# Two re-orderings in a twelve-sublayer kernel: the next layer's statistics behind the turned probabilities, and the next rows turned between the two columns of the second expert product

## The chip, the cores and the metric

The kernel runs as one program on one core of a Trainium2 chip. The metric is the device time of one execution in microseconds (us). TensorE (PE) multiplies matrices, VectorE (DVE), ScalarE (ACT) and GpSimd (POOL) do elementwise work, and SyncE (SP) issues the DMA transfers. The engines run their own instruction streams in order and meet through semaphores. PEld is the loading of TensorE's stationary operand.

## The reference, cut to what matters

Twelve sublayers are added one after another to x, which has 64 x 32 = 2048 rows of 256 features. Two of them matter here. The fixed experts (sublayer 2) normalise x twice, project it, and send each row through one of eight expert networks, chosen by the row's position:

```python
x = x + _L0_ffn_ref(_layernorm(x, axis=-1), ...)    # sublayer 2, in words:
# f = normalised x;  a = f + attn_w(norm(f) * ln_scale + ln_bias) + attn_b
# h = gelu(a @ w1[e] + b1[e]);  o = h @ w2[e] + b2[e];  x += gelu(o @ next_w + next_b)
```

The complex attention (sublayer 4) is self-attention among the 32 rows of each of the 64 batches, with scores from products folded ahead of time:

```python
x = x + _L1_attn_ref(_layernorm(x, axis=-1), ...)   # sublayer 4, in words:
# t = xn @ m;  s = t xn^T + biases;  p = exp(scale*(s - max s));  z = xn @ n
# x += (p @ z) / sum(p) + output bias
```

Sublayer 5 begins with a layer norm of x again. Its mean and root are made row tile by row tile inside sublayer 4; these are the "next layer's statistics" of the title.

## The kernel before, in words

All of x lies in SBUF as 16 tiles of 128 rows. The sublayers run one after another, with a barrier and a new block of engine programs between two of them. Inside a sublayer every engine has a function `turn`, written out by hand, that is called for the first and the last tiles in straight code and for the others in a hardware loop. What stands first in a turn is done first on that engine, whatever is ready, so the order of the calls in `turn` is the schedule.

**Fixed experts** (`fixed_experts_ffn`, names begin with `l0f_`). A turn handles one of 8 experts, with two row tiles (u = 0 and 1) of 128 rows. In the turn of expert e, TensorE does the first layer of e (`first_layer`, 16 products into `ps_h`), turns the normalised rows of e+1 to features (`turn_normed`, four transposes for each u, all into one PSUM bank `ps_t`), does the second layer of e (`second_layer`, 16 products into `ps_e`: 8 for each of two 128-column halves oc), the projection of e+1 (`projection`, into `ps_a`) and the next projection of e (`next_projection`, into `ps_y`). ScalarE copies the turned rows out of `ps_t` (`keep_turned`, into `flatT` and `xn2T`), makes the gelus (`gelus`) and copies the second layer's output (`keep_expert_output`, into `eoT`). The bank `ps_t` is shared by u = 0 and u = 1, so `turn_normed(n, 1)` waits for `keep_turned(n, 0)`. `projection` waits for `keep_turned(n, 1)`. `next_projection` waits for `eoT`. VectorE makes `xaT` from the projection, and `first_layer` of the next turn waits for it.

**Complex attention** (`complex_attention`, names begin with `l1a_`). A turn handles one of 16 row tiles. TensorE in turn i: scores of tile i (`scores`), transposes of tile i+2 (`turn_xn`), projections of tile i+1, and the weighed rows of tile i (`weighed_rows`, which waits for the probabilities that VectorE has turned). VectorE in turn i: row maxima of the scores, statistics of the finished tile i-1 for the next layer (`next_norm`), statistics of tile i+3 (`norm_stats`), turned probabilities of tile i (`turn_probs`, after ScalarE's exp), the normalised tile i+3 (`normed`, which waits for the root that GpSimd makes from `norm_stats`), and the sum into x (`add_output`). GpSimd makes that root (`layer_norm_root`), then x plus bias, then the next layer's root (`next_root`) from what `next_norm` left. `normed` gives the tile that `turn_xn` transposes.

```python
wait(dve, s["x_done"], n)
nc.vector.bn_stats(next_stats[:], core.x[:, i, :]).then_inc(s["next_stats_ready"], 1)
after(dve, s["next_rstd_ready"], n - 1, alone=True)
wait(dve, s["next_stats_ready"], n)
nc.vector.bn_aggr(next_moments[:], next_stats[:]).then_inc(s["next_mean_ready"], 1)
```

Of the kernel before, what the change touches and what calls it, by code (L numbers as in the profile page):

```python
# [25 lines left out]
P = 128  # L26
D = 256
C = D // P
# [1169 lines left out]
def complex_attention(core, tag):  # L1198
# [4 lines left out]
    nc = core.nc  # L1203
# [4 lines left out]
    with ExitStack() as ctx:  # L1208
# [231 lines left out]
        @block.vector  # L1440
        def _(dve):
            def spread_bv():
                nc.vector.tensor_copy(bv_rows[:], bv.unsqueeze(2).broadcast_to([P, CE, P])).then_inc(s["bv_spread"], 1)

            def keep_products():
                dve.wait_ge(s["vectors_ready"], 1)
                nc.vector.tensor_copy(bias_product[:], ps_c)
                nc.vector.tensor_copy(u[:], ps_u)
                nc.vector.tensor_copy(w[:], ps_w).then_inc(s["vectors_kept"], 1)
                dve.wait_ge(s["n_ready"], 1)  # L1450
                nc.vector.tensor_copy(n_vo[:], ps_n[:]).then_inc(s["n_kept"], 1)

            def keep_output_bias():
                dve.wait_ge(s["output_bias_ready"], 1)
                nc.vector.tensor_tensor(output_bias[:], ps_bo, bo, ALU.add).then_inc(s["output_bias"], 1)

            def maxima(n):
                dve.wait_ge(s["scores_ready"], n)
                nc.vector.tensor_reduce(big[:], ps_s, X, ALU.max, negate=True).then_inc(s["max_ready"], 1)
                dve.wait_ge(s["max_ready"], n)  # L1460
                nc.vector.tensor_scalar(minus_big[:], big[:], float(scale), None, ALU.mult).then_inc(s["bias_ready"], 1)

            def turn_probs(n):
                dve.wait_ge(s["exp_ready"], n)

                after(dve, s["y_ready"], n - 1)
                nc.vector.transpose(probsT[:], probs[:]).then_inc(s["probs_turned"], 1)

                after(dve, s["x_done"], n - 1)
                nc.vector.reciprocal(rinv[:], rsum[:]).then_inc(s["inv_ready"], 1)  # L1470

            def add_output(i, n):
                dve.wait_ge(s["y_ready"], n)
                dve.wait_ge(s["x_biased"], n)
                dve.wait_ge(s["inv_ready"], n)
                nc.vector.scalar_tensor_tensor(core.x[:, i, :], ps_y, rinv[:], x_plus_bo[:], ALU.mult,
                                               ALU.add).then_inc(s["x_done"], 1)

            def next_norm(i, n):
# [7 lines that stand above are left out]
            def turn(i, par):  # L1487
                if there(i, 0):
                    maxima(i + 1)
                if there(i, -1):  # L1490
                    next_norm(i - 1, i)
                if there(i, 3):
                    norm_stats(dve, nc, s, i + 4, core.x[:, i + 3, :], stats[:], mean[:])
                if there(i, 0):
                    turn_probs(i + 1)
                if there(i, 3):

                    after(dve, s["xn_turned"], i + 3)
                    normed(dve, nc, s, i + 4, core.x[:, i + 3, :], xn[:], mean[:], rstd[:])
                if is_turn(i, -AHEAD):  # L1500
                    core.wait_for_pack(dve)
                    spread_bv()
                if is_turn(i, -2):
                    keep_products()
                if is_turn(i, -1):
                    keep_output_bias()
                if there(i, 0):
                    add_output(i, i + 1)

            all_turns(dve, turn)  # L1510
            next_norm(NT - 1, NT)

# [522 lines left out]
def fixed_experts_ffn(core, tag):  # L2035
# [3 lines left out]
    nc = core.nc  # L2039
    E, HID = 8, 4 * D  # L2040
    HC = HID // P
# [3 lines left out]
    with ExitStack() as ctx:  # L2045
# [56 lines left out]
        @block.tensor  # L2102
        def _(pe):
            def turn_normed(n, u):

                if u:
                    pe.wait_ge(half_read[u - 1], n)
                    pe.wait_ge(flat_read[u - 1], n)
                else:
                    after(pe, half_read[U - 1], n - 1)  # L2110
                    after(pe, flat_read[U - 1], n - 1)
                pe.wait_ge(ln[1][u]["xn_ready"], n)
                for c in range(C):
                    nc.tensor.transpose(ps_t[:, c, :], flat[:, u, c * P:c * P + P], ident)
                for c in range(C):
                    last = nc.tensor.transpose(ps_t[:, C + c, :], xn2[:, u, c * P:c * P + P], ident)
                last.then_inc(turned[u], 1)

            def projection(n):
                after(pe, s["xaT_ready"], n - 1)  # L2120
                pe.wait_ge(half_read[U - 1], n)
                for oc in range(C):
                    for c in range(C):
                        last = nc.tensor.matmul(ps_a[:, oc, :], attn_w[:, c, oc * P:oc * P + P], xn2T[:, c, :],
                                                start=(c == 0), stop=(c == C - 1))
                last.then_inc(s["attn_ready"], 1)

            def first_layer(n):
                pe.wait_ge(s["w1_loaded"], n * 32)
                pe.wait_ge(s["xaT_ready"], n)  # L2130
                for k in range(HC // 2):
                    after(pe, h_kept[k], n - 1)
                    for hc in (2 * k, 2 * k + 1):
                        for c in range(C):
                            last = nc.tensor.matmul(ps_h[:, k, hc % 2, :], w1[:, c, hc * P:hc * P + P], xaT[:, c, :],
                                                    start=(c == 0), stop=(c == C - 1))
                    last.then_inc(h_ready[k], 1)

            def second_layer(n):
                pe.wait_ge(s["w2_loaded"], n * 32)  # L2140
                after(pe, s["eoT_ready"], n - 1)
                for oc in range(C):
                    for hc in range(HC):
                        if oc == 0 and hc % 2 == 0:
                            pe.wait_ge(h_kept[hc // 2], n)
                        last = nc.tensor.matmul(ps_e[:, oc, :], w2[:, hc, oc * P:oc * P + P], hT[:, hc, :],
                                                start=(hc == 0), stop=(hc == HC - 1))
                last.then_inc(s["out_ready"], 1)

            def next_projection(n):  # L2150
                after(pe, s["y_kept"], n - 1)
                pe.wait_ge(s["eoT_ready"], n)
                for u in range(U):
                    for c in range(C):
                        last = nc.tensor.matmul(ps_y[:, u, :], eoT[:, c, u * P:u * P + P], next_w[:, c, :],
                                                start=(c == 0), stop=(c == C - 1))
                last.then_inc(s["y_ready"], 1)

            def turn(e, now, ahead, ahead2):
                if ahead and not now:  # L2160
                    core.wait_for_pack(pe)
                if now:
                    first_layer(e + 1)
                if ahead:
                    turn_normed(e + 2, 0)
                if now:
                    second_layer(e + 1)
                if ahead:
                    turn_normed(e + 2, 1)
                    projection(e + 2)  # L2170
                if now:
                    next_projection(e + 1)

            staged_tiles(pe, turn, E)

        @block.scalar
        def _(act):
# [40 lines left out]
            def turn(e, now, ahead, ahead2):  # L2218
                if now:
                    gelus(e + 1)  # L2220
                if ahead:
                    keep_turned(e + 2, 0)
                if now:
                    keep_expert_output(e + 1)
                if ahead:
                    keep_turned(e + 2, 1)
                if now:
                    act.wait_ge(s["y_kept"], e + 1)
                    nc.scalar.activation(y[:], y[:], ACT.Gelu).then_inc(s["gelu_ready"], 1)

# [1570 lines left out]
```

## Time and profile before

| what | value |
|---|---|
| time before, median of 3 runs | 3566.3 us (3560.57 to 3572.57) |
| the profiled execution, its own time | 3571.8 us |
| its span | 3570.0 us |
| PE busy in the span | 3298.9 us (92%) |
| PE weight loads | 2646.9 us (74%) |
| DVE busy | 2152.4 us (60%) |
| ACT busy | 1428.5 us (40%) |
| POOL busy | 1017.6 us (29%) |
| mean granted TensorE clock | 0.958 |

The profiled execution took 3571.8 us, of which 1.8 us lie outside its span. It is 5.5 us above the median of the runs. Shares are averages over twelve stages with different limits; the steady part of the fixed experts lies at about 375 to 517 us of the span, and that of the complex attention at about 1012 to 1073 us. Times in rows are in us from the span's start. A granted clock of 1.00 is TensorE's level of 2.4 GHz, 0.50 that of 1.2 GHz.

### The profile page before, as it was taken

To read this page: it belongs to the slowest core of one execution; us is meant where nothing else is said; L and a number is where in the kernel's file an instruction comes from. 1 tells how busy PE (TensorE), PEld (TensorE's weight loads), DVE (VectorE), ACT (ScalarE), POOL (GpSimd) and SP (SyncE) were. 2 spreads that over 40 slices of the span, in tenths; PEclk is the share of its full clock that TensorE was granted. 3 is DMA by queue.
4 is the path that set the end of the run, shared out by engine and by line. 5 is a ranking of instruction groups with operands and counts; after the bars stand their busy time and mean duration, and the time that the engine had idled before them with its cause. 6 is when DMAs were issued, how large, how long until landed. Compare 5 with 4: busy or idle time off the path is not lost. (4 is left out here: it accounts for less than half of the span.)

```text
span 3570.0 us, 105629 instructions
## 1 busy us (share of the span) xinstructions
PE 3298.9 (92%) x39322; PEld 2646.9 (74%) x39322; DVE 2152.4 (60%) x7124; ACT 1428.5 (40%) x4209; POOL 1017.6 (29%) x1587
## 2 busy tenths in 40 slices
PE   8988889999986999999999999887999999998799
PEld 6767777777765888888877777774666788878576
DVE  3766225555656888889645555763334566558545
ACT  2334335555532333333245555541111455555222
POOL 0112113333342444445333333442110111112421
PEclk9999999999997999999999999978999999999799
DMA  6653334212103000000041111033112411110323
GB/s 208 216 175 154 102 94 108 61 56 56 64 1 140 3 3 3 2 3 2 2 99 43 40 47 46 2 111 124 46 47 72 87 38 38 41 34 2 108 79 114
DMA packets 149258, 238.26 MB, mean 67 GB/s; under 512 B 14456, under 2 KB 121720, under 8 KB 147176
## 3 DMA queue, kind: packets, MB, share of 16 engines
q1 hardware_dynamic: 138816, 203.16, 18.2%
q0 software_dynamic: 10176, 31.47, 3.1%
q8 instruction: 177, 2.90, 0.4%
q14 instruction: 89, 0.73, 0.1%
HBM read 213.61 MB, written 38.94 MB: 71 GB/s over the span
## 5 line engine op out<-in xcount | busy, mean ns | idle before, releaser
L3299 POOL TENSOR_TENSOR l1fu_second_weighed<-l1fu_second,l1fu_parts 128x256 bf16<-128x256 bf16 x384 | 278.7, 753 | 339.2 <-DVE l1fu_second L3540 332.3
L3351 PEld LDWEIGHTS l1fu_ps_u<-l1f_xnT_all,l1f_key_in 128*128 128x128 f32 x2048 | 252.0, 195 | 17.3 <-issue 11.0
L3351 PE MATMUL l1fu_ps_u<-l1f_xnT_all,l1f_key_in 128*128 (+1 forms) x2048 | 254.9, 278 | 8.6 <-issue 5.5
L3362 PE MATMUL l1fu_ps_y<-l1f_key_out,l1fu_units 128*128 128x256 f32 x1024 | 250.6, 389 | 2.0 <-DVE l1fu_units L3548 2.0
L3362 PEld LDWEIGHTS l1fu_ps_y<-l1f_key_out,l1fu_units 128*128 128x128 f32 x1024 | 185.7, 190 | 33.6 <-issue 6.2
L3413 ACT COPY l1fu_plane<-l1fu_ps_p 128x512 f32<-128x512 f32 x128 | 75.1, 586 | 250.4 <-PE l1fu_ps_p L3341 250.4
L3535 DVE TENSOR_TENSOR l1fu_first<-l1fu_index,l1fu_counted 128x1024 bf16<-128x1024 bf16 x128 | 166.8, 1303 | 12.8 <-PE l1fu_ps_p L3341 9.6
L3421 ACT ACTIVATE l1fu_units<-l1fu_ps_u 128x512 f32<-128x512 f32 x128 | 76.6, 598 | 151.9 <-PE l1fu_ps_y L3362 139.9
L1020 ACT ACTIVATE l3x_scores<-l3x_scores,l3x_minus_big 128x257 f32<-128x257 f32 x256 | 129.0, 511 | 2.3 <-DVE l3x_minus_big L1109 2.3
L1020 ACT ACTIVATE l1x_scores<-l1x_scores,l1x_minus_big 128x257 f32<-128x257 f32 x256 | 128.9, 511 | 2.1 <-DVE l1x_minus_big L1109 2.1
L1020 ACT ACTIVATE l2x_scores<-l2x_scores,l2x_minus_big 128x257 f32<-128x257 f32 x256 | 128.8, 511 | 2.1 <-DVE l2x_minus_big L1109 2.1
L3007 DVE TENSOR_TENSOR l2f_hidden<-l2f_hidden,l2f_ps_u 128x512 f32<-128x512 f32 x55 | 37.8, 688 | 151.7 <-PE l2f_ps_u L2751 136.8
L3341 PE MATMUL l1fu_ps_p<-l1fu_second_weighed,l1fu_first 64*128 64x32 bf16 x6144 | 113.1, 191 | 10.2 <-POOL l1fu_second_weighed L3299 9.4
L854 PE MATMUL l2x_ps_kv<-weights,l2x_ctx_sb 128*128 128x256 f32 x488 | 121.6, 392 | 0.0
L854 PE MATMUL l3x_ps_kv<-weights,l3x_ctx_sb 128*128 128x256 f32 x488 | 121.6, 392 | 0.0
L854 PE MATMUL l1x_ps_kv<-weights,l1x_ctx_sb 128*128 128x256 f32 x488 | 121.6, 392 | 0.0
L844 PE MATMUL l2x_ps_kv<-l2x_ctx_sb,weights 128*128 128x256 f32 x496 | 119.1, 383 | 0.0
L844 PE MATMUL l3x_ps_kv<-l3x_ctx_sb,weights 128*128 128x256 f32 x496 | 118.6, 382 | 0.0
L844 PE MATMUL l1x_ps_kv<-l1x_ctx_sb,weights 128*128 128x256 f32 x496 | 118.4, 382 | 0.0
L3341 PEld LDWEIGHTS l1fu_ps_p<-l1fu_second_weighed,l1fu_first 64*128 64x128 bf16 x6144 | 98.3, 95 | 26.5 <-issue 12.9
L854 PEld LDWEIGHTS l3x_ps_kv<-weights,l3x_ctx_sb 128*128 128x128 f32 x488 | 87.7, 189 | 33.0 <-ACT l3x_kT L1013 12.0
L854 PEld LDWEIGHTS l2x_ps_kv<-weights,l2x_ctx_sb 128*128 128x128 f32 x488 | 87.7, 189 | 33.0 <-issue 12.0
(743 smaller groups left out, 8383.6 us busy)
## 6 DMA issues: line engine op xcount, KB each, us to landing
rows_by_expert<-in_zeros_dram SPq DMA_DIRECT2D x1, 17544.0 KB
l0x_ctxT<-in_ctx_T_dram SPq DMA_DIRECT2D x32, 514.0 KB, 5.2
l0x_ctx_rows<-in_ctx_dram SPq DMA_DIRECT2D x64, 256.0 KB, 3.3
l0f_w<-in_L_ffn_w_dram SPq DMA_DIRECT2D x16, 1024.0 KB, 5.2
l1x_ctx_sb<-in_ctx_T_dram SPq DMA_DIRECT2D x64, 256.0 KB, 2.8
l2x_ctx_sb<-in_ctx_T_dram SPq DMA_DIRECT2D x64, 256.0 KB, 2.8
l3x_ctx_sb<-in_ctx_T_dram SPq DMA_DIRECT2D x64, 256.0 KB, 2.8
l1x_mask_raw<-in_mask_int_dram SPq DMA_DIRECT2D x16, 514.0 KB, 3.9
```

The costliest lines, as they stand in the source:

```text
L844: last = nc.tensor.matmul(dst[:, oc, :], wt["k"][:, c, oc * P:oc * P + P], ctx_sb[:, b, c, :], start=(c == 0), stop=(c == C - 1))
L854: last = nc.tensor.matmul(dst[:, kc, :], ctx_sb[:, b, c, kc * P:kc * P + P], wt["v"][:, c, :], start=(c == 0), stop=(c == C - 1))
L1020: last = nc.scalar.activation(scores[:, b, r, :], scores[:, b, r, :], ACT.Exp, bias=minus_big[:, b, r:r + 1], accum_out=rsum[:, b, r:r + 1])
L3007: nc.vector.tensor_tensor(hidden[:, n % 2, 0:w.hidden], hidden[:, n % 2, 0:w.hidden], ps_u[:, 0:w.hidden], ALU.mult).then_inc(s["hidden_re ...
L3299: last = nc.gpsimd.tensor_tensor(second_weighed[:, k % 2, part], second[:, k % 2], parts[:, 1 - par, part, TC * k:TC * k + TC].unsqueeze(2 ...
L3341: last = nc.tensor.matmul(ps_p[:, half, :, token], first[rows, k % 2, token, :], second_weighed[rows, k % 2, part, token, :], start=(part ...
L3351: last = nc.tensor.matmul(ps_u[:, k % 2, j, :], key_in[:, c, JS * k + j, :], xnT_all[:, c, bass.ts(tile, P)], start=(c == 0), stop=(c == C ...
L3362: last = nc.tensor.matmul(ps_y, units[:, k, j, :], key_out[:, JS * k + j, :], start=(k + j == 0), stop=(k == K - 1 and j == JS - 1))
L3413: nc.scalar.copy(plane[:, par].rearrange("p j (h n) -> p h j n", h=2)[:, :, :, TC * k:TC * k + TC], ps_p).then_inc(s["plane_kept"], 1)
L3421: nc.scalar.activation(units[:, k], ps_u[:, k % 2], ACT.Gelu).then_inc(s["activated"], 1)
L3535: nc.vector.tensor_tensor(first[:, k % 2], index[:, par, TC * k:TC * k + TC].unsqueeze(2).broadcast_to([P, TC, P]), counted[:].unsqueeze(1 ...
```

## The change

Two independent edits, each only an order of calls.

In the complex attention, VectorE calls `next_norm(i - 1, i)` after `turn_probs(i + 1)` and not before `norm_stats`. In the fixed experts, `second_layer` is split into its two column halves, and TensorE turns the second row tile of the next expert between them; ScalarE copies these turned rows before it copies the expert's output.

```diff
             def turn(i, par):
                 if there(i, 0):
                     maxima(i + 1)
-                if there(i, -1):
-                    next_norm(i - 1, i)
                 if there(i, 3):
                     norm_stats(dve, nc, s, i + 4, core.x[:, i + 3, :], stats[:], mean[:])
                 if there(i, 0):
                     turn_probs(i + 1)
+                if there(i, -1):
+                    next_norm(i - 1, i)
                 if there(i, 3):
@@ fixed experts, TensorE
-            def second_layer(n):
-                pe.wait_ge(s["w2_loaded"], n * 32)
-                after(pe, s["eoT_ready"], n - 1)
-                for oc in range(C):
-                    for hc in range(HC):
-                        if oc == 0 and hc % 2 == 0:
-                            pe.wait_ge(h_kept[hc // 2], n)
-                        last = nc.tensor.matmul(ps_e[:, oc, :], w2[:, hc, oc * P:oc * P + P], hT[:, hc, :],
-                                                start=(hc == 0), stop=(hc == HC - 1))
-                last.then_inc(s["out_ready"], 1)
+            def second_layer(n, oc):
+                if oc == 0:
+                    pe.wait_ge(s["w2_loaded"], n * 32)
+                    after(pe, s["eoT_ready"], n - 1)
+                for hc in range(HC):
+                    if oc == 0 and hc % 2 == 0:
+                        pe.wait_ge(h_kept[hc // 2], n)
+                    last = nc.tensor.matmul(ps_e[:, oc, :], w2[:, hc, oc * P:oc * P + P], hT[:, hc, :],
+                                            start=(hc == 0), stop=(hc == HC - 1))
+                if oc == C - 1:
+                    last.then_inc(s["out_ready"], 1)
@@ turn
                 if ahead:
                     turn_normed(e + 2, 0)
                 if now:
-                    second_layer(e + 1)
+                    second_layer(e + 1, 0)
                 if ahead:
                     turn_normed(e + 2, 1)
+                if now:
+                    second_layer(e + 1, 1)
+                if ahead:
                     projection(e + 2)
                 if now:
                     next_projection(e + 1)
@@ fixed experts, ScalarE, turn
                     gelus(e + 1)
                 if ahead:
                     keep_turned(e + 2, 0)
+                    keep_turned(e + 2, 1)
                 if now:
                     keep_expert_output(e + 1)
-                if ahead:
-                    keep_turned(e + 2, 1)
-                if now:
                     act.wait_ge(s["y_kept"], e + 1)
```

VectorE in one turn of the complex attention, in the straight code ahead of its loop; rows with a sign are of before (-) or of the changed kernel (+).

```order
 L1459 TENSOR_REDUCE l1a_big<-l1a_ps_s 128x1
 L1461 TENSOR_SCALAR l1a_minus_big<-l1a_big 128x1
-L1482 BN_STATS l1a_next_stats<-x_sb 128x6
-L1485 BN_AGGR l1a_next_moments<-l1a_next_stats 128x2
 L200 BN_STATS l1a_stats<-x_sb 128x6
 L202 BN_AGGR l1a_mean<-l1a_stats 128x2
 L1467 STREAM_TRANSPOSE l1a_probsT<-l1a_probs 128x32
 L1470 RECIPROCAL l1a_rinv<-l1a_rsum 128x1
+L1482 BN_STATS l1a_next_stats<-x_sb 128x6
+L1485 BN_AGGR l1a_next_moments<-l1a_next_stats 128x2
 L208 TENSOR_SCALAR l1a_xn<-x_sb,l1a_mean,l1a_rstd 128x256
 L1476 SCALAR_TENSOR_TENSOR x_sb<-l1a_ps_y,l1a_rinv,l1a_x_plus_bo 128x256
```

The pair for the next layer (`next_norm`, L1482 and L1485) has moved from ahead of the tile's own pair (L200, L202) to between the reciprocal and the normalised tile (L208).

TensorE in the loop of the fixed experts, from the first turned tile of a turn to its next projection.

```order
 L2114 MATMUL l0f_ps_t<-const,l0f_flat 128x128 x2
 L2116 MATMUL l0f_ps_t<-const,l0f_xn 128x128 x2
-L2146 MATMUL l0f_ps_e<-l0f_hT,l0f_w 128x256 x16
+L2146 MATMUL l0f_ps_e<-l0f_hT,l0f_w 128x256 x8
 L2114 MATMUL l0f_ps_t<-const,l0f_flat 128x128 x2
 L2116 MATMUL l0f_ps_t<-const,l0f_xn 128x128 x2
+L2146 MATMUL l0f_ps_e<-l0f_hT,l0f_w 128x256 x8
 L2124 MATMUL l0f_ps_a<-l0f_xn2T,weights_0 128x256 x4
-L2155 MATMUL l0f_ps_y<-weights_0,l0f_eoT 128x256 x4
+L2156 MATMUL l0f_ps_y<-weights_0,l0f_eoT 128x256 x4
```

The second turned tile now has eight products of the second layer behind it before the projection (L2124) that reads it. From here on line numbers of the changed kernel are one to four higher.

ScalarE in the same loop, before:

```order
L2187 COPY l0f_flatT<-l0f_ps_t 128x128 x2
L2190 ACTIVATE l0f_xn2T<-l0f_ps_t,weights_0 128x128 x2
L2213 ACTIVATE l0f_eoT<-l0f_ps_e,l0f_b 128x256 x2
L2187 COPY l0f_flatT<-l0f_ps_t 128x128 x2
L2190 ACTIVATE l0f_xn2T<-l0f_ps_t,weights_0 128x128 x2
```

and in the changed kernel:

```order
L2191 COPY l0f_flatT<-l0f_ps_t 128x128 x2
L2194 ACTIVATE l0f_xn2T<-l0f_ps_t,weights_0 128x128 x2
L2191 COPY l0f_flatT<-l0f_ps_t 128x128 x2
L2194 ACTIVATE l0f_xn2T<-l0f_ps_t,weights_0 128x128 x2
L2217 ACTIVATE l0f_eoT<-l0f_ps_e,l0f_b 128x256 x2
```

The copy of the expert's output (`eoT`) went from between the two copies of turned rows to behind both.

## Rows read from the trace of the kernel before

**Rows 1.** Windows view: the stretch, its length, busy time (x instructions) by engine, clock, DMA

```profile
core 0: us, PE busy (x) PEld busy (x) DVE busy (x) ACT busy (x) POOL busy (x), PEclk, DMA share, GB/s
375.37:395.64 20.27, 18.37 (x90) 16.00 (x89) 5.61 (x17) 7.11 (x20) 3.22 (x8) 1.00 0.34 105
1012.02:1015.43 3.41, 3.41 (x65) 2.53 (x57) 2.26 (x8) 1.65 (x6) 1.46 (x3) 1.00 0.02 5
1015.43:1019.12 3.69, 3.50 (x66) 2.56 (x57) 2.35 (x11) 1.65 (x6) 1.69 (x5) 1.00 0.00 0
1019.12:1064.04 44.92, 39.19 (x616) 28.23 (x616) 30.56 (x111) 19.05 (x66) 26.76 (x67) 1.00 0.00 1
1062.44:1066.18 3.74, 3.46 (x57) 2.54 (x57) 2.21 (x8) 1.70 (x6) 3.37 (x9) 1.00 0.03 7
1090.00:1100.00 10.00, 10.00 (x49) 10.00 (x49) 0.00 (x0) 1.01 (x1) 0.00 (x0) 0.50 1.02 433
```

**Rows 2.** Waits view, fixed experts: total us, times, longest

```profile
PE l0f_ps_a L2124 <- ACT l0f_xn2T L2190: 13.6, 7, 2.0
```

**Rows 3.** Timeline of one expert's turn: start, us, engine, line [idle before]

```profile
395.64 7.07 PE L2146 MATMUL l0f_ps_e<-l0f_hT,l0f_w 128*128 128x256 f32 x32
...
396.76 0.82 ACT L2190 ACTIVATE l0f_xn2T<-l0f_ps_t,weights 128x128 f32<-128x128 f32 x2
...
402.77 0.38 PE L2116 MATMUL l0f_ps_t<-const,l0f_xn 128*128 128x128 f32 x2
402.81 0.84 ACT L2213 ACTIVATE l0f_eoT<-l0f_ps_e,l0f_b 128x256 f32<-128x256 f32 x2 [5.23 <-issue]
...
404.14 0.82 ACT L2190 ACTIVATE l0f_xn2T<-l0f_ps_t,weights 128x128 f32<-128x128 f32 x2
...
405.11 1.97 PE L2124 MATMUL l0f_ps_a<-l0f_xn2T,weights 128*128 128x256 f32 x8 [1.96 <-ACT l0f_xn2T L2190]
...
406.91 1.89 PE L2155 MATMUL l0f_ps_y<-weights,l0f_eoT 128*128 128x256 f32 x8
407.20 0.88 DVE L2256 SCALAR_TENSOR_TENSOR l0f_xaT<-l0f_ps_a,weights,l0f_flatT 128x256 f32<-128x256 f32 x2 [11.26 <-PE l0f_ps_a L2124]
```

**Rows 4.** Timeline of one turn of the complex attention

```profile
1040.02 0.57 POOL L1290 TENSOR_TENSOR next_rstd<-l1a_next_moments,const 128x1 f32 x1 [0.22 <-POOL l1a_next_moments L1287]
1040.02 0.18 DVE L1459 TENSOR_REDUCE l1a_big<-l1a_ps_s 128x1 f32<-128x32 f32 x1
...
1040.32 0.43 DVE L1482 BATCH_NORM_STATS2 l1a_next_stats<-x_sb 128x6 f32 x1
...
1040.68 0.19 ACT L1407 ACTIVATION_READ_ACCUMULATOR l1a_probs<-l1a_ps_s,l1a_minus_big 128x1 f32 x1
...
1040.98 0.43 DVE L200 BATCH_NORM_STATS2 l1a_stats<-x_sb 128x6 f32 x1
...
1041.51 0.18 DVE L202 BATCH_NORM_AGGREGATE l1a_mean<-l1a_stats 128x2 f32<-128x6 f32 x1
1041.61 0.21 DVE L1467 STREAM_TRANSPOSE l1a_probsT<-l1a_probs 128x32 f32<-128x32 f32 x1
...
1042.16 0.57 POOL L167 TENSOR_TENSOR l1a_rstd<-l1a_mean,const 128x1 f32<-128x1 f32 x1
...
1042.84 0.74 DVE L208 TENSOR_SCALAR l1a_xn<-x_sb,l1a_mean,l1a_rstd 128x256 f32 x1 [0.96 <-POOL l1a_rstd L167]
...
1043.63 0.44 PE L1330 MATMUL l1a_ps_t<-const,l1a_xn 128*128 128x128 f32 x2 [0.18 <-DVE l1a_xn L208]
...
1044.02 0.18 DVE L1459 TENSOR_REDUCE l1a_big<-l1a_ps_s 128x1 f32<-128x32 f32 x1
```

**Rows 5.** Waits view, 1019 to 1066 us

```profile
PEld l1a_ps_y L1367 <- issue: 7.7, 11, 0.8
...
PEld l1a_ps_t L1330 <- DVE l1a_xn L208: 2.8, 10, 0.3
```

**Rows 6.** Operation view of the first layer's products: min/median/max ns, first and last start

```profile
L2135 PE MATMUL l0f_ps_h<-l0f_xaT,l0f_w x256: 379/379/765, 365.7 to 517.0; 128*128 128x256 f32 x128
```

## The prediction, made before the changed kernel ran

> **What bounds the kernel now.** I read the page first: TensorE is busy for nine tenths of the span, so a gain has to come from stretches in which it waits. The chain that ended last covers only the last sublayer and tells nothing of the two edited stages. So I read each stage's timeline, and the windows view to see how much of a turn TensorE is idle.
>
> Fixed experts: one turn takes 20.27 us, of which TensorE is busy 18.37, at a granted clock of 1.00 [rows 1]. The missing 1.90 us are one wait: the projection (L2124) waits for ScalarE's copy of the second turned row tile, 7 times, 13.6 us in all [rows 2]. The timeline shows why. The transposes of the second tile end at 403.15 (402.77 + 0.38). ScalarE has just begun the expert's output at 402.81 and copies the turned rows behind it, until 404.96 (404.14 + 0.82). The projection starts at 405.11 with 1.96 us idle before it [rows 3]. No other engine is near full: ScalarE 7.11, VectorE 5.61 of 20.27 us [rows 1].
>
> Complex attention: 11 turns take 44.92 us, 4.08 each, with VectorE busy 30.56 and TensorE 39.19 us [rows 1]. Neither is full. What closes the loop is VectorE and GpSimd in turns. From one row maximum (1040.02) to the next (1044.02) VectorE goes without a pause but one, 0.96 us, in which `normed` (L208) waits for GpSimd's root of the tile's own statistics [rows 4]. These statistics (L200, L202) stand behind `next_norm`, so its time lies on the chain maximum, statistics, root, normalised tile, sum, maximum. TensorE waits for this chain twice in a turn: for the normalised tile before its transposes (1043.63 in rows 4; 2.8 us over 10 turns) and before the weighed rows (7.7 us over 11 turns, put down to issue, partly the wait for the turned probabilities) [rows 5].
>
> **The change, part by part.** No edit adds or removes an instruction of work. The same transposes, products and copies run, and no DMA moves.
>
> *Fixed experts.* The second tile is turned after the first eight products of the second layer. These take half of 7.07 us, so from 395.64 they end near 399.2. The bank `ps_t` has to be read by then: ScalarE ends its copies of the first tile at 397.58 (396.76 + 0.82), 1.6 us early [rows 3]. With half a microsecond of transposes and 1.3 us of copies (from 403.65, the end of the output's activation, to 404.96 before) `xn2T` is complete near 401.0. TensorE comes to the projection when all its earlier work is done, at 403.15 as now. So 2.1 us of cover are there, and the wait is gone: 7 x 1.9 us, the 13.6 us of [rows 2].
>
> What is late next? The second layer now ends at 403.15 and not half a microsecond earlier, and `eoT` follows it by 0.84 us and some 0.1 us of semaphore: ready near 404.1. `next_projection` needs it when the projection is done, 1.80 us after its start (406.91 - 405.11), near 404.95: 0.85 us of cover [rows 3]. The first layer of the next turn needs `xaT`, which ends at 408.08 (407.20 + 0.88), while the next projection runs until 408.80; this relation is unchanged [rows 3]. ScalarE in front of `keep_expert_output` now waits for the second turned tile, early in the second column; nothing but the output is queued behind. The norms of the following expert are counted from the next projection and stay where they were relative to the first layer. The idle of a turn is 1.90 us in all, so there is no more to gain: 13.3 to 13.6 us. I take 13.6.
>
> *Complex attention.* `next_norm` costs VectorE 0.66 us from its start to that of the next pair (1040.32 to 1040.98) [rows 4]. With the tile's own statistics ahead of it, GpSimd begins the root 0.66 us sooner. Then the turned probabilities can start at 1040.95 instead of 1041.61, and the exp they need ends at 1040.87 (1040.68 + 0.19) [rows 4]: it just doesn't hold them. `next_norm` comes into the gap of 0.96 us in which VectorE waits for the root: 0.66 fits with 0.3 us to spare, if the exp is not late. GpSimd's last step for the next layer (L1290) ends at 1040.59, so the semaphore that `next_norm` waits for between its two instructions is set long before its new place.
>
> The chain is then 4.08 - 0.66 = 3.42 us long. TensorE's own length of a turn is shown by the first turn, in which `next_norm` has no tile yet: 3.41 us from transpose to transpose, TensorE busy in all of them [rows 1]. This is the floor. Two loops of equal length hold each other up now and then, so I take 3.45 us. That is 44.92 - 11 x 3.45 = 7.0 us for the 11 turns, 0.24 for the turn before them (3.69) and 0.29 for the one behind (3.74) [rows 1]: 7.5 us. The floor would give 8.0 us. If `next_norm` ended 0.3 us behind the root in each turn, a turn would take 3.7 us: 44.92 - 40.7, 4.2 us. At the very end of the stage `next_norm` of the last tile stays last; nothing to gain there.
>
> A contention to weigh: at its new place `next_norm` runs beside GpSimd's root. Before, L1482 (from 1040.32, 0.43 us) already ran beside GpSimd's power (L1290, 1040.02 to 1040.59, 0.57 us), and both took what their twins L200 (0.43) and L167 (0.57) take [rows 4]. By this row nothing is added. The Trainium skill (SBUF — State Buffer, section SBUF: two separate sides) says that VectorE and GpSimd share one pair of ports under an exclusive lock, and that the loser is blocked for the whole instruction. If the statistics took that lock, the root would be held up to 0.43 us in 12 turns, 5 us, and the whole gain would be 16 us instead of 21. The trace of before speaks against it for this pair.
>
> **Sum.** 13.6 + 7.5 = 21.1 us. The profiled execution of 3571.8 us would take 3550.7. It lies 5.5 us above the median of the runs (3566.3), so the median should be 3545.2 us, 0.6% less.
>
> **The rivals.**
> 1. *The attention turn becomes bound by VectorE.* The exp or the root beside `next_norm` is late, and `normed` starts behind `next_norm`. For it: only 0.3 us to spare, and 0.08 us at the exp [rows 4]. Against: the first turn ran at TensorE's pace. Then 4.2 us instead of 7.5: gain 17.8, 3548.5 us. Chance 0.15.
> 2. *The attention gains nothing*, as another wait of 0.6 us in the ring replaces it. Gain 13.6, 3552.7 us. Chance 0.07.
> 3. *The fixed experts' edit doesn't do what it says*: the projection waits as long for something else (`eoT` was the only neighbour I found, with 0.85 us of cover). Then only 7.5 us: 3558.8 us, within what can be measured. Chance 0.05.
> 4. *Slower, by TensorE's clock.* Where a stage begins, the granted clock can be at the 1.2 GHz level: from 1090 to 1100 us it is 0.50 although TensorE is busy in all of the 10 us [rows 1]. A product then takes up to 765 ns instead of 379 [rows 6], so each microsecond at that level loses about half. All later stages now start 13.6 or 21 us sooner, and the stretches at the low level may come out longer. From 42 us of additional low level the gain of 21.1 is gone, from 64 us the kernel is 0.3% slower. Nothing in the two edited loops, both at 1.00, points to it. Chance 0.04. The Trainium skill (TensorE: Matmul & The Clock Gate, Part 1) says that a warm, busy engine keeps the full rate; by that alone this rival would be empty, but the row at 1090 us shows full activity at the low level.
>
> **How the numbers follow.** The forecast has the remaining 0.69. Runs of one kernel spread over 12 us (3560.57 to 3572.57), 0.3%, or 10.7 us, which is about what a measurement can tell from no change. The forecast's own size is a gain of 17.5 to 21.6 us with the bounds of the attention turn; the spread adds 6 us on either side. The range of 3537 to 3557 us takes this in, with rivals 1 and 2; it leaves out 3 and 4 and some of the spread. Faster by over 0.3%: the forecast and rival 1 (0.84) and about half to two thirds of rival 2, 0.88 in all; within 0.3%: 0.08; slower: 0.04.
>
> **What the changed profile would show.** Fixed experts: the wait of L2124 for `xn2T` gone from the waits, a turn of 18.4 us, TensorE idle under 0.1 us in it, `eoT` in time for L2156. Complex attention: 3.45 us a turn; L1482 inside what was the 0.96 us gap; the root starting 0.66 us sooner after the maximum; TensorE's wait before its transposes gone. All durations unchanged. I would be wrong if L2156 waited for `eoT`, if L1482 lengthened GpSimd's root, or if L208 waited for nothing but started later than the root allows.

## The result, and the profile after

The changed kernel takes 3531.94 us (median of 6 runs, 3528.72 to 3544.53) against 3564.9 us for the kernel before (median of 6). The ratio is 0.9909, 95% interval 0.9892 to 0.9927: 33.0 us faster where 21.1 were forecast, and below the lower end of the range (3537). By the interval the gain is 26 to 38.5 us, so a gain of 21.1 is excluded, while one at the lower end of the range (28 us) is not. The profiled execution took 3532.03 us. Four of the later runs, of 3862 to 7314 us, were disturbed and are left out of every number.

Both edits did what they were meant to do. Here is the windows view of the changed kernel. Its lines are one expert's turn, seven of them, the complex attention from the second turn's transposes to the last (twelve turns), and the products at the attention's head (stretch, length, then busy time of PE, PEld, DVE, ACT, POOL, the granted clock, DMA):

```profile
367.26:385.41 18.15, 18.15 (x91) 15.99 (x90) 5.61 (x17) 7.11 (x20) 3.22 (x8) 1.00 0.36 117
367.26:493.84 126.58, 126.58 (x614) 111.48 (x613) 38.25 (x107) 49.51 (x133) 19.30 (x48) 1.00 0.36 117
987.68:1028.64 40.96, 40.96 (x681) 30.43 (x673) 34.25 (x121) 19.79 (x72) 28.53 (x72) 1.00 0.00 1
967.40:978.41 11.01, 11.01 (x73) 10.03 (x74) 1.87 (x6) 0.58 (x1) 1.57 (x4) 1.00 0.01 1
```

The same stretches of the kernel before:

```profile
375.37:517.21 141.84, 128.22 (x614) 111.66 (x613) 38.26 (x107) 49.59 (x133) 19.28 (x48) 1.00 0.33 104
1015.43:1064.04 48.61, 42.69 (x682) 30.78 (x672) 32.92 (x121) 20.71 (x72) 28.45 (x71) 1.00 0.00 1
990.24:1006.16 15.92, 15.92 (x73) 13.66 (x74) 1.88 (x6) 0.59 (x1) 1.57 (x4) 0.68 0.00 1
```

What to see: in both edited loops TensorE is now busy in the whole stretch. Seven turns of the experts lost 15.3 us (141.84 - 126.58) and twelve of the attention 7.65 us (48.61 - 40.96). The last lines show something else. The products at the attention's head are the same 72 or so instructions in both kernels, no edit touches them, and they take 4.9 us less, at a clock of 1.00 instead of 0.68.

The timeline of an expert's turn, to be read beside [rows 3]:

```profile
370.94 0.38 PE L2116 MATMUL l0f_ps_t<-const,l0f_xn 128*128 128x128 f32 x2
...
371.15 3.62 PE L2146 MATMUL l0f_ps_e<-l0f_hT,l0f_w 128*128 128x256 f32 x16
371.41 0.43 ACT L2191 COPY l0f_flatT<-l0f_ps_t 128x128 f32<-128x128 f32 x2 [2.23 <-PE l0f_ps_t L2116]
371.73 0.82 ACT L2194 ACTIVATE l0f_xn2T<-l0f_ps_t,weights 128x128 f32<-128x128 f32 x2
...
374.61 1.89 PE L2124 MATMUL l0f_ps_a<-l0f_xn2T,weights 128*128 128x256 f32 x8
374.81 0.84 ACT L2217 ACTIVATE l0f_eoT<-l0f_ps_e,l0f_b 128x256 f32<-128x256 f32 x2 [2.26 <-PE l0f_ps_e L2146]
...
376.34 1.89 PE L2156 MATMUL l0f_ps_y<-weights,l0f_eoT 128*128 128x256 f32 x8
```

The copies of the second tile end at 372.55 under the second column, and the projection starts without a wait. `eoT` is complete at 375.65, 0.7 us ahead of the next projection.

The timeline of one attention turn, to be read beside [rows 4]:

```profile
1015.13 0.19 DVE L1459 TENSOR_REDUCE l1a_big<-l1a_ps_s 128x1 f32<-128x32 f32 x1
...
1015.48 0.43 DVE L200 BATCH_NORM_STATS2 l1a_stats<-x_sb 128x6 f32 x1
1016.01 0.18 DVE L202 BATCH_NORM_AGGREGATE l1a_mean<-l1a_stats 128x2 f32<-128x6 f32 x1
1016.15 0.21 DVE L1467 STREAM_TRANSPOSE l1a_probsT<-l1a_probs 128x32 f32<-128x32 f32 x1
...
1016.32 0.41 DVE L1482 BATCH_NORM_STATS2 l1a_next_stats<-x_sb 128x6 f32 x1
...
1016.66 0.57 POOL L167 TENSOR_TENSOR l1a_rstd<-l1a_mean,const 128x1 f32<-128x1 f32 x1
1016.83 0.18 DVE L1485 BATCH_NORM_AGGREGATE l1a_next_moments<-l1a_next_stats 128x2 f32<-128x6 f32 x1
...
1017.34 0.73 DVE L208 TENSOR_SCALAR l1a_xn<-x_sb,l1a_mean,l1a_rstd 128x256 f32 x1 [0.33 <-POOL l1a_rstd L167]
...
1018.40 0.33 PE L1330 MATMUL l1a_ps_t<-const,l1a_xn 128*128 128x128 f32 x1
```

`next_norm` (L1482, L1485) lies in the gap, which has 0.33 us left. It runs beside GpSimd's root, which still takes 0.57 us and starts 1.53 us after the row maximum; before it was 2.14 us. From 987.68 to 1028.64 the transposes come every 3.41 us, the floor named in the prediction.

**Where the rest is.** The two loops give 15.3 + 7.65 = 22.9 us, and with the last turns of the attention some 23 us. The two profiles differ by 39.7 us, the medians by 33.0; the profiled execution of before was itself 6.9 us above its median. So about 10 us of the median's gain, give or take the 6 us of its interval, lie outside the edited loops. The attention's head shows one kind of time that can differ there. I use one number for it, called the level time below: the time at the 1.2 GHz level, 2 x (1 - granted clock) x time. It can be worked out so because the traces have only the two granted clocks 1.00 and 0.50. Each run's mean granted clock gives it. In the two profiles of this comparison it is 302 us (before) and 270 us (changed).

### The profile page after: what moved, and what is told of

Same layout as the page of the kernel before. It is cut to its first block and busy times, and to the rows that moved or that the text cites. A ratio compares the mean times of both kernels' runs of the same rounds, so it can differ in the third digit from the quotient of the medians.

```text
span 3530.3 us, 105624 instructions
## 1 busy us (share of the span) xinstructions
PE 3281.2 (93%) x39322; PEld 2634.0 (75%) x39322; DVE 2153.7 (61%) x7124; ACT 1426.2 (40%) x4209; POOL 1017.9 (29%) x1587
## 5 line engine op out<-in xcount | busy, mean ns | idle before, releaser
L3343 PE MATMUL l1fu_ps_p<-l1fu_second_weighed,l1fu_first 64*128 64x32 bf16 x6144 | 113.1, 191 | 11.5 <-POOL l1fu_second_weighed L3301 10.3
L1104 DVE CUSTOM_DVE_ANT_0 l2x_scores<-l2x_ps_s,l2x_bias 128x257 f32<-128x257 f32 x256 | 93.7, 422 | 31.0 <-PE l2x_ps_s L869 30.8
```

The lines of the kernel that those rows point to most:

```text
L1104: last = nc.vector.tensor_tensor_reduce(scores[:, b, r], ps_s[:, r, 0:KEYS], bias[:, b] if mask else bias[:], 1.0, MASKED, ALU.add, ALU.ma ...
L3343: last = nc.tensor.matmul(ps_p[:, half, :, token], first[rows, k % 2, token, :], second_weighed[rows, k % 2, part, token, :], start=(part ...
```

## The experiments

They ran on four chips, on each of which the kernel before takes 3510 to 3515 us, some 50 us less than in the first comparison. The table gives the medians' ratio, the number of runs n, the means, and the mean level time, worked out as above run by run. The standard error of a mean is 1.5 to 3 us (about 1 for before), and that of a level time 2 to 7 us (2 to 3 for before). Times in us.

| kernel | ratio (95%) | n | mean | before, mean (n) | level time | before's level time |
|---|---|---|---|---|---|---|
| e1 attention only | 0.9979 (0.9966 to 0.9992) | 12 | 3505.2 | 3512.9 (25) | 235 | 236 |
| e2 experts only | 0.9952 (0.9934 to 0.9970) | 8 | 3495.8 | 3512.9 | 231 | 236 |
| e3 before again | 0.9998 (0.9986 to 1.0009) | 12 | 3512.7 | 3512.9 | 235 | 236 |
| e4 changed, again | 0.9909 (0.9892 to 0.9925) | 6 | 3482.7 | 3512.9 | 218 | 236 |
| e5 before, two delays | 1.0005 (0.9993 to 1.0017) | 12 | 3514.8 | 3512.6 (23) | 233 | 237 |
| e6 changed, two delays | 0.9938 (0.9923 to 0.9954) | 6 | 3494.1 | 3512.6 | 248 | 237 |
| e7 before, mixed products | 1.0002 (0.9990 to 1.0015) | 11 | 3514.0 | 3512.6 | 241 | 237 |
| e8 changed, mixed products | 0.9923 (0.9908 to 0.9939) | 6 | 3487.5 | 3512.6 | 224 | 237 |
| e9 changed, third | 0.9932 (0.9916 to 0.9949) | 6 | 3484.5 | 3509.8 (14) | 221 | 231 |
| e10 changed, first delay | 0.9952 (0.9935 to 0.9969) | 8 | 3491.8 | 3509.8 | 235 | 231 |
| e11 changed, second delay | 0.9956 (0.9938 to 0.9974) | 6 | 3492.1 | 3509.8 | 234 | 231 |
| e12 changed, narrow last | 0.9912 (0.9897 to 0.9928) | 6 | 3483.6 | 3514.2 (9) | 223 | 242 |

### One edit alone: e1 and e2

e1 has only `next_norm` moved, e2 only the experts' order.

```diff
 # e1: the kernel before with
-                if there(i, -1):
-                    next_norm(i - 1, i)
                 if there(i, 3):
                     norm_stats(...)
                 if there(i, 0):
                     turn_probs(i + 1)
+                if there(i, -1):
+                    next_norm(i - 1, i)
 # e2: the changed kernel with this taken back
```

> Only the first edit: next_norm behind turn_probs in the complex attention; the fixed experts as before. If the gain lies in the edited loops, each by itself (A), the time is 7.8 us under the kernel before, which is what the stage shortened by between the two profiles (a ratio of 0.998), with 3.41 us a turn. If the gain beyond the loops (33.0 us by medians against 23.0 us in the two loops) comes with this edit and not with the other (B), it is 15 to 18 us under. Rival C, that the rest is the granted clock falling out by chance in a few runs: 8 us give or take 4, with the stages outside the attention differing by as much between two runs of one kernel as between kernels.

> Only the second edit: the second row tile turned between the two columns in the fixed experts; the attention as before. A: 15.2 us under the kernel before, by the stage's length in the two profiles (ratio 0.996), with 18.15 us a turn. B, in which the rest comes with this edit: about 25 us under. C: 15 us give or take 4.

By means, e1 is 7.8 us faster and e2 17.1 us. Within their errors of 2 and 3 us these are the lengths that the loops lost (8 and 15). In the profiles the attention stage, from its first instruction to the next stage's, takes 74.1 us in e1 against 82.0 us in e2, which has the old order and whose head also ran at full clock: 7.9 us for the edit at equal clock. The experts' stage takes 164.4 us in e2, 179.3 in e1. So A holds for each edit alone. The errors of 2 and 3 us can't exclude that one of them brings a part of the extra; e1's own B (15 to 18 us) is excluded, and e2's (25 us) is 8 us away.

### Each kernel once more: e3 and e4

> The kernel before once more, unchanged, as a second profile of it. A and C: the same time within 0.2%, and the stages ahead of the first edit, 8.2 us longer in the profile of before than in that of the changed kernel, differ by some us between the two profiles of the same kernel as well, with the time at the 1.2 GHz level. B, that the changed kernel makes unchanged stages faster: the stages ahead of the first edit are as long as in the first profile of before, within 1 us.

> The changed kernel once more, as a second profile and a second estimate of its ratio. A and C: the gain moves from 33 towards 23 us (ratio 0.9935). B: it stays at 33 us (0.9909), and the stages ahead of the first edit stay as short as in the first profile of the changed kernel.

e3 is equal to before. e4 is 30.2 us faster by means, 7 us more than the loops, with an error of 2.4 us, so the extra was not only an accident of the first comparison. In its profile the experts' stage takes 164.4 us and the attention's 79.0, because its head was slow, as in the first profile of before. e1 and e2 together give 24.9 us; the difference from 30.2 is 5.3 us with an error of 4, so it is not shown that the extra needs both edits. The level time of e4 is 218 us against 236 us for before, 18 us less with an error of 3.5. That of e1 (235) and e2 (231) has errors of 5 and 6 us.

The two sublayers ahead of the experts hold the same code in every kernel. They were 8.2 us longer in the first profile of before (350.8 us) than in that of the changed kernel (342.6). In e3 they take 354.4 us, in e5 and e7, whose code there is before's too, 342.1 and 346.0, and in e4 346.1. So these 8.2 us were the draw of the profiled execution, and B is refuted for these stages. Whether the changed kernel makes unchanged stages faster can be seen in the means alone, by the level time.

### Two idle stretches: e5 and e6

The output doesn't change; idle time for TensorE is added between two stages. By the profiles the first delay of e6 costs 1.2 us and the second 1.3; those of e5 cost 1.8 and 1.6.

```diff
 # fixed experts, VectorE, behind its last turn (e6; e5: also flatT, so three)
             staged_tiles(dve, turn, E)
+            for scratch in (xn2, flat):
+                nc.vector.tensor_tensor(scratch[:], y[:], y[:], ALU.add)
 # complex attention, GpSimd, behind its last root (e6; e5: 256 and 256)
             next_root(NT - 1, NT)
+            for k, width in enumerate((256, 128)):
+                nc.gpsimd.tensor_tensor(x_plus_bo[:, 0:width], core.x[:, 0, 0:width], output_bias[:, 0:width],
+                                        ALU.add).then_inc(s["x_biased"], 1)
+                pool.wait_ge(s["x_biased"], NT + 1 + k)
```

> The kernel before with two idle stretches put in: at the end of the fixed experts VectorE adds y to itself three times into scratch tiles (some 1.9 us by the 0.69 us of one such operation), at the end of the complex attention GpSimd adds 256 columns twice into a tile that is no longer read (some 1.8 us). Output unchanged. The two delays are meant to bring the later stages to the places relative to the clock's own steps that they have in the changed kernel. Theory P (the 7 to 9 us beyond the loops come from where the stages fall against the steps of the granted clock): the time at the 1.2 GHz level falls from 236 us (mean of 25 runs of the kernel before on this chip) towards 218 us (changed kernel), so the kernel is not 3.7 us slower but 3 to 6 us faster than before. Rival Q (these microseconds belong to the edits themselves, or to chance): level time stays at 236 us and the kernel is 3 to 4 us slower.

> The changed kernel with two delays that should bring the later stages back to where the kernel before has them: VectorE adds y to itself twice (some 1.3 us) at the end of the fixed experts, GpSimd 256 and 128 columns (some 1.3 us) at the end of the complex attention. Output unchanged. P: the time at the low level rises from 218 towards 236 us and the gain against before falls from 31 us to 21 - 2.6, some 19 to 22 us (ratio 0.994). Q: the gain falls by the 2.6 us alone, to 27 to 30 us (ratio 0.992).

e6 came out as P says in its sign: the attention stage grew by 1.3 us (80.3 against 79.0 in e4, both with a slow head), but the kernel by 11.5 us against e4, and the level time rose from 218 to 248 us, 12 more than P said. Q's 27 to 30 us of gain are excluded; it is 18.4 us, with an error of 2.4, a little under P's 19 to 22. e5 did not come out as P says: it is 2.3 us slower than before by means and not faster, which is within its error of 1.8 us what its own delays cost (3.4), as Q says. Its level time is 233 us, with an error of 3, against 237. The extra can be taken away by delays, but my guess of the delays that would give it to the kernel before was wrong.

### Which delay: e9, e10 and e11

e10 has the first of e6's delays alone, e11 the second, e9 none.

> The changed kernel a third time, beside the two that follow. If the gain beyond the loops is lasting, 30 to 33 us under before (ratio 0.991) with some 218 us at the low level; if the first two were lucky draws, 23 to 26 us (0.993) with some 235 us.

> The changed kernel with the first delay alone: VectorE adds y to itself twice (1.3 us) at the end of the fixed experts. If the places of the stages between the two edits (the attention's head above all) decide, the rise of the low time seen with both delays comes with this one, and the gain falls to 20 to 23 us. If the stages behind the attention decide, the gain falls by the 1.3 us only, to some 30 us.

> The changed kernel with the second delay alone: GpSimd adds 256 and 128 columns (1.3 us) at the end of the complex attention. The other way round: 30 us of gain left if the stages between the edits decide, 20 to 23 us if those behind the attention do.

e9 lies between its two cases: 25.3 us by means, 26.7 by medians, with 221 us at the low level. With either delay the kernel gains 7 us less, of which 1.2 or 1.3 us are the delay itself; the error of each difference is 3 us. Either alone brings the level time to 234 or 235 us and leaves 18 us of gain.

The two expectations made one mistake: a delay ahead of the attention moves the stages behind it as well. So the first delay doesn't test the stages between the edits alone. The second does part them: in e11 everything ahead of it is as in the changed kernel, and the extra is gone all the same. Both results, then, are what follows if the stages behind the attention decide. The profiles of e10 and e11 can't show it, for they were taken in executions that lost nothing (3484.4 and 3485.1 us, e9's is 3482.0). Without a delay the changed kernel has a level time of 218 and 221 us (e4, e9). With one edit undone or with a delay it is 231 to 248 us, but with errors of 3 to 7 us each.

### The order of the products at the attention's head: e7, e8 and e12

```diff
 # e7 and e8, the lines taken out in short
-                [m, both columns] [narrow u and w, both] [narrow c] [n, both columns]
+                m_column(0)
+                vectors(0)
+                m_column(1).then_inc(s["m_ready"], 1)
+                vectors(1)
+                n_column(0)
+                last = over_features(ps_c, ...)
+                last.then_inc(s["vectors_ready"], 1)
+                n_column(1).then_inc(s["n_ready"], 1)
 # e12: m, both; n, both; then all of the narrow ones
```

> The kernel before, with only the order of TensorE's weight products at the head of the complex attention changed: the 40 narrow products (1 to 32 columns wide) stand between the wide ones (256 columns) and not in one block behind the first 16. In two profiles of the kernel before the granted clock fell to 0.5 in and behind this block and the stage took 86.7 us; in one kernel with the same attention it did not and took 82.0. P1 (the block of narrow products is what lets the clock fall): the head runs at 1.00, the time at the low level falls by up to 10 us and the kernel is 3 to 5 us faster. P2 (any start of a stage can fall so, whatever the order): no change beyond 2 us, with low stretches at the head in the profile as before.

> The changed kernel with the same mixed order of weight products. If P1 holds and the changed kernel usually escapes the fall already, it is as fast as the changed kernel (31 us under before) or up to 2 us faster; if it escapes it only half of the time, 33 us. P2: 31 us under before, no difference.

> The changed kernel with the 40 narrow products at the head of the complex attention behind all 32 wide ones. If the block of narrow products is where the clock falls and the wide ones behind it pay for it (18.8 against 13.9 us of the head in two profiles), the head takes 13.9 to 15.5 us wherever the stage starts, and the kernel is 1 to 3 us faster than the changed one (28 to 33 us under before, ratio 0.991 to 0.992). If the low level comes with the start of a stage and not with the narrow block, the head is as often 18 to 19 us long as before and the time is that of the changed kernel, 25 to 31 us under before.

None helps beyond the error. e7 is equal to before, and e8 (25.1 us faster than before) no faster than the changed kernel. Here is TensorE's timeline at the head (start, us), of the kernel before:

```profile
990.24 5.38 PE L1300 MATMUL l1a_ps_m<-weights 128*128 128x256 f32 x16 [1.93 <-PEq L3675]
995.45 4.81 PE L1300 MATMUL l1a_ps_b<-weights 128*128 128x1 f32 x40
1000.19 6.13 PE L1300 MATMUL l1a_ps_n<-weights 128*128 128x256 f32 x16
```

of the changed kernel:

```profile
967.40 3.69 PE L1300 MATMUL l1a_ps_m<-weights 128*128 128x256 f32 x16 [1.93 <-PEq L3677]
970.93 3.99 PE L1300 MATMUL l1a_ps_b<-weights 128*128 128x1 f32 x40
974.85 3.72 PE L1300 MATMUL l1a_ps_n<-weights 128*128 128x256 f32 x16
```

of e7, with mixed products:

```profile
983.08 2.81 PE L1300 MATMUL l1a_ps_m<-weights 128*128 128x256 f32 x8 [1.92 <-PEq L3682]
985.67 3.46 PE L1300 MATMUL l1a_ps_b<-weights 128*128 128x1 f32 x16
988.95 3.76 PE L1300 MATMUL l1a_ps_m<-weights 128*128 128x256 f32 x8
992.50 3.46 PE L1300 MATMUL l1a_ps_b<-weights 128*128 128x1 f32 x16
995.77 3.76 PE L1300 MATMUL l1a_ps_n<-weights 128*128 128x256 f32 x8
```

and of e12, narrow products last:

```profile
968.88 5.38 PE L1300 MATMUL l1a_ps_m<-weights 128*128 128x256 f32 x16 [1.93 <-PEq L3677]
974.10 3.62 PE L1300 MATMUL l1a_ps_n<-weights 128*128 128x256 f32 x16
977.55 4.81 PE L1300 MATMUL l1a_ps_b<-weights 128*128 128x1 f32 x40
```

The same 16 wide products take 3.7 us or 6.1, and 8 of them 3.76 at the low level. In e7 the low level held on through the mixed order, from 984.1 to 1001.1, and its attention stage was the longest of all, 90.1 us. In e8, with the same order, it held for 6.8 us only (973.3 to 980.1). With the narrow block last (e12) the wide `n` products escape (3.62 us), but the first block still pays (5.38) and the narrow ones at the end do (4.81 us). Where the clock falls is seen in the windows view, before:

```profile
990.24:991.40 1.16, 1.16 (x6) 1.03 (x7) 0.61 (x2) 0.00 (x0) 0.23 (x1) 1.00 0.05 14
991.40:994.80 3.40, 3.40 (x10) 2.69 (x9) 1.27 (x4) 0.00 (x0) 1.34 (x3) 0.51 0.00 0
995.45:998.30 2.85, 2.85 (x28) 2.85 (x26) 0.00 (x0) 0.59 (x1) 0.00 (x0) 0.99 0.00 0
998.30:1000.19 1.89, 1.89 (x16) 1.71 (x15) 0.00 (x0) 0.00 (x0) 0.00 (x0) 0.50 0.00 0
```

and in e12:

```profile
974.10:977.55 3.45, 3.45 (x18) 3.04 (x16) 0.00 (x0) 0.59 (x1) 0.00 (x0) 1.00 0.00 0
977.55:980.40 2.85, 2.85 (x28) 2.85 (x26) 0.00 (x0) 0.00 (x0) 0.00 (x0) 0.99 0.00 0
980.40:982.29 1.89, 1.89 (x17) 1.71 (x16) 0.00 (x0) 0.00 (x0) 0.00 (x0) 0.50 0.00 0
```

The clock falls twice. The first fall comes 1.2 us after the first wide product, ahead of every narrow one, in before as in e12. So P1 is refuted as the whole cause: the narrow block is not needed for the clock to fall. The second fall comes 2.85 us after the first narrow product in both, though the block stands 3.5 us later in e12. For this fall the narrow products remain a suspect, which no run here settles. They are not enough by themselves either: in five of the profiles (the first of the changed kernel, e1, e2, e9, e11) the head has the narrow block in the middle and no fall at all. e12 is 30.6 us faster than before by means, the changed kernel 25 to 30, a difference that these runs can't tell; no version beats it clearly.

## Why the prediction was right in its mechanisms and too small in its number

- **Fixed experts, right.** The wait is gone, all covers held (`eoT` with 0.7 us, forecast 0.85; `xn2T` with 2.06, forecast 2.1). The term was mis-sized a little: 15.3 us for 13.6. I had counted only the idle time before the projection, and said that there was no more to gain. TensorE's busy time in a turn fell as well, from 18.37 to 18.15 us. Before the wait, the last transpose ends with nothing beside it, 0.38 us after its start where the next one starts after 0.22 (382.27 and 382.49); behind the wait, the projection takes 1.97 us where it now takes 1.89. Together that is 0.24 us, about the 0.22 by which the busy time fell.
- **Complex attention, right.** 3.41 us a turn where 3.45 was taken, 8 us for 7.5. `next_norm` fitted into the gap with 0.33 us left (forecast 0.3). Rivals 1, 2 and 3 did not come.
- **The contention, right.** GpSimd's root beside `next_norm` still takes 0.57 us, and L1482 and L1485 take 0.41 and 0.18 us beside it. The Trainium skill (SBUF — State Buffer, section SBUF: two separate sides) ties the lock to VectorE operations in a two-port mode or with two SBUF inputs, a condition that the prediction left out. The statistics read one input, and neither engine was held up here.
- **The step that failed** is the sum: "13.6 + 7.5 = 21.1 us" has no term for TensorE's clock outside the edited loops. I had the effect, but as rival 4 and with one sign: "the stretches at the low level may come out longer". They came out shorter, by 10 to 18 us (236 to 218, 231 to 221). At the attention's head 10.2 us more at the low level cost 4.9 us (2 x 0.32 x 15.92, and 15.92 against 11.01), so 10 to 18 us are worth, by estimate, 5 to 9. With the loops' 23 that is 28 to 32 us, and the two means and two medians of this kernel in e4 and e9 were 25.3 to 32.4. A range that took in the clock with both signs would have reached down to about 3530.
- **The size of the miss.** The time forecast, 3545.2 us, was 13.3 us too long. Of these 1.7 us are the experts' term and up to 0.4 the attention's. 1.4 us come from the starting point, as the median of before is 3564.9 us by six runs where three gave 3566.3. The rest, near 10 us, has no term in the sum. How much of it the first comparison drew by luck is not known: 7 and 2 us beyond the loops were found again (e4, e9).
- The likeliest case of the forecast (faster by over 0.3%, chance 0.88) came.

**What stays open.** It is shown that the changed kernel gains more than its loops (30.2 and 25.3 us by means, for 23), that its level time is then lower, and that delays of 1.2 to 2.5 us take the extra away (18.4, 18.0 and 17.8 us in e6, e10 and e11). Which stages give it is not shown; e11 points at those behind the attention. The profiles don't place it, as the low stretches change between two executions of one kernel: the attention's stage takes 74.1 us in two profiles of the changed kernel and 79.0 in the third. Why a fixed shift should lower the mean over many executions, and not only the time of one, stays open too. Nor can I say beforehand which delay is a good one; e5 shows that.

## What to carry to other kernels

When an order is moved, look for the gap in which the moved work can lie (here 0.96 us for 0.66) and for the floor that another engine sets (here 3.41 us, read from the one turn that lacked the work): the result fell on the floor. And when a profile shows stage heads at the low clock level, give every edit that shifts them a term of either sign, here up to 9 us in 3500. Judge an edit by the length of its own loop. Of the 33 us here only 23 are seen in the edited loops, and a later edit that moves a stage by 1 us may take the rest back, as e10 and e11 did. And when a wait is to go, count more than its idle time: here 1.9 us of idle time were worth 2.2 us a turn, as the work on both sides of it no longer ran back to back.

## What the runs showed of the hardware that I had not expected

- The same products of 256 columns ran at either level with TensorE busy in all of the time: the head of the attention took 15.92 us at a mean clock of 0.68 or 11.01 at 1.00, both with busy shares of 100%. In e7 TensorE was busy in all of the 19.28 us of its head at a mean clock of 0.56.
- A delay of about 1.2 us that one engine makes between two stages cost 7 us of program time, itself included, with an error of 3 us (e10, e11 against e9).
- The same kernel took 52 us less in e3 than in the first comparison (3513.1 and 3564.9, medians). By the profiles the difference lies in the two sorted experts' stages (376.5 and 236.4 us from their first gathered rows to the next stage's start or the end, against 351.6 and 211.8), not in the stages of this change.
